# Gate and up projections of a routed feed-forward: scaled tokens, or coefficients applied to unscaled pieces

## The chip, the cores and the metric

The kernel runs on one NeuronCore of one Trainium2 chip. The metric is the device time of the program in microseconds (us). Each kernel is run several times and the median counts; one further execution is profiled. The engines are TensorE (PE in the profile, its weight loads PEld), VectorE (DVE), ScalarE (ACT), GpSimd (POOL) and SyncE (SP), which here only issues DMAs. PE writes to PSUM, which has eight banks of 512 fp32 columns.

## The reference

Two layers work on x (8 batches of 64 tokens of width 256, 512 tokens in all) with a context of 8 x 1601 rows. Each layer has cross-attention to the context, then (layer 0) a small attention and a top-1 routed ffn, or (layer 1) a state-space scan with gelu and a top-2 routed feed-forward. The change is in the last one:

```python
def _moe_linear(x, router_w, expert_w):
    logits = x @ router_w.T
    vals, idx = jax.lax.top_k(logits, K)
    probs = jax.nn.softmax(vals, axis=-1)
    onehot = jax.nn.one_hot(idx, n_exp, dtype=x.dtype)
    combine = jnp.einsum('tk,tke->te', probs, onehot)
    for e in range(n_exp):
        out = out + combine[:, e:e + 1] * (x @ expert_w[e].T)
g = _moe_linear(xt, router_gate, w_gate)      # 8 experts, 256 -> 1024
u = _moe_linear(xt, router_up, w_up)          # 8 experts, 256 -> 1024
inter = jax.nn.silu(g) * u
d = _moe_linear(inter, router_down, w_down)   # 8 experts, 1024 -> 256
```

All eight experts are computed for all tokens; the combine coefficient is zero for those not chosen.

## The kernel before

Semaphores are written out by hand, and each engine has its own in-order program. Precision is kept by splitting operands into a high and a low fp16 part (`wh`, `wl` for weights, times 256), and three matmuls stand for one product: high x high, high x low, low x high.

Attention runs over 16 groups g (8 batches in each of 2 layers), each with 13 steps k, one per 128 context rows. PE's units of a step stand in `STEP_UNITS`: S is the score of the step, P a bound on the maximum, K and V the projections of the next or own batch, W the weighing of values two steps back. ACT takes the exponentials of the scores (L1103), DVE the maxima (L1346). Group 15, the last, has no next batch, so its steps hold S, W and its own V units only. Between the units, `events(g, k)` puts the single operations of the middle work (output projection, norms, small attention, ffn of layer 0, scan, routers) of each tile of 128 tokens: `MID` and `SSM` name the operation for each step counted from step `MID_START` = 6 of a tile's first group. The scan's gelu (`s_y`) needs another ACT function table than the exponential, so two table loads stand around it. The last token tile (t = 3) can only follow group 15: its chain stands in `TAIL`.

The routed feed-forward of layer 1:
- `scale_tokens` (POOL, L649) multiplies the tokens of a tile by the coefficient of an expert; `transpose_tokens` (PE, L824) turns them; `split_tokens` (ACT L1121, DVE L1380) makes the fp16 parts `xch`, `xcl`. This is done for 2 routers x 8 experts x 4 tiles, in the 40 items of `X`.
- A unit (r, it) is gate (r = 0) or up (r = 1) for 128 of the 1024 output columns: weights are stationary, 512 tokens move, and the 8 experts with 2 halves of 256 and 3 products add up in one PSUM bank, 48 matmuls. Four gate units are done in parts ahead of the last tile, in the gaps of its chain (`gate_part`, items g and d of `TAIL`); the other 12 run in the loop at L995.
- `inner` (ACT, L1253) and the loop at L1595 (DVE) form silu from PSUM: exp, add one, reciprocal, times gate, times up; ACT and POOL (L711) split the result into `ih`, `il`, which have the intermediate columns on partitions as the down product wants them.
- Each weight block is 1 MB, loaded by SP to one of three buffers `w32` and split by ACT (`wh`, L1118) and DVE (`wl`, L1377) into a ring of four.
- Down: for each expert and tile 24 matmuls of 256 columns (L1031); DVE adds them into x with the coefficient (L1630).

PE's matmuls nearly all go through one helper, L717.

Of the kernel before, what the change touches and what calls it, by code (L numbers as in the profile page):

```python
# [7 lines left out]
F16 = mybir.dt.float16  # L8
# [8 lines left out]
B = 8  # L17
# [65 lines left out]
MID_START = 6  # L83
# [26 lines left out]
GATE_PARTS = [(n, e, *tiles) for units, tiles in (((0, 1), (0, 2)), ((0, 1), (2, 3)), ((2,), (0, 2)), ((2,), (2, 3)),  # L110
                                                  ((3,), (0, 2)), ((3,), (2, 3))) for n in units for e in range(E)]
LAST_GATE_PARTS = [(n, e, 3, 4) for n in range(GATES) for e in range(E)]

TAIL = ("x5 g g x6 y5 g y6 g x7 g y7 h2 out x8 h3 g g g g g y8 s_norm s_turn l2 g s_u x9 g s_0 y9 x10 g s_1 y10 x11 g "
        "s_2 y11 x12 g s_3 y12 x13 g s_4 y13 x14 g s_5 y14 x15 s_y y15 x16 g g g g g_stats y16 x17 g g g g g_norm "
        "g g g g g_parts g_clean m_stats y17 g g g g g m_norm m_turn l3 g r_logits g g g g g g g g g g g r_pick").split()
for e in range(E):
    TAIL += ["g"] * min(2, len(GATE_PARTS) - TAIL.count("g")) + [f"x{X_THIRD + e}", f"y{X_THIRD + e}"]  # L120
TAIL += ["g"] * (len(GATE_PARTS) - TAIL.count("g"))
TOKENS_AT = dict(zip((1, 3, 5, 7, 9, 15, 17, 19, 21, 23, 25, 27, 29, 30), range(X_BOTH, len(X))))
for n in range(len(LAST_GATE_PARTS)):
    TAIL.append("d")
    if n in TOKENS_AT:
        TAIL += [f"x{TOKENS_AT[n]}", f"y{TOKENS_AT[n]}"]
    if n == 9:
        TAIL += [f"h{GATES}", f"l{GATES}"]
for w in range(GATES + 1, 2 * GATES):
    TAIL += [f"h{w}", f"l{w}"]  # L130

UNITS = [(0, it) for it in range(GATES)] + [(1, it) for it in range(GATES)] + \
        [(r, it) for it in range(GATES, IT) for r in range(2)]
W_RING = 4


def events(g, k):
# [135 lines left out]
def build(nc, d, out):  # L273
    with ExitStack() as ctx:
# [18 lines left out]
        with ExitStack() as s:  # L293
            xg = sb(s, "xg", [P, 2, 2, D])
# [9 lines left out]
        small = sb(ctx, "small", [P, 32])  # L304
# [17 lines left out]
        SM_IOTA, SM_MIX, SM_HEAD, SM_FOLD = 2, 10, 18, 24  # L322
# [28 lines left out]
        with ExitStack() as s:  # L351
# [6 lines left out]
            xm = sb(s, "xm", [P, TT, D])  # L358
# [1346 lines left out]
```

## Time and profile before

| | before |
|---|---|
| time, median of 3 runs | 997.72 us (995.42 to 998.7) |
| profiled execution, its own time | 995.52 us |
| its span, first to last instruction | 993.7 us |
| PE / DVE / ACT / POOL busy | 925.3 / 606.9 / 535.0 / 202.1 us |
| mean granted TensorE clock | 0.986 |
| HBM read, written | 64.88 MB, 17.32 MB |

The profile gives busy time by engine, groups of instructions by line and shape, the chain of waits that ended last, and timelines. A matmul's record ends when its result is out, so consecutive matmuls overlap in the records: their price is the distance between starts. PEclk or clock is the granted TensorE clock as a share of 2.4 GHz; 0.5 is 1.2 GHz.

### The profile page before, as it was taken

What the parts mean: (1) busy time and instruction counts of PE and PEld (TensorE: products, weight loads), DVE (VectorE), ACT (ScalarE), POOL (GpSimd) and SP (SyncE); (2) the same over time, 40 slices, a digit from 0 to 9 for tenths busy, and PEclk for the clock granted to TensorE, in tenths of its full rate; (3) what the DMA queues carried; (4) which work ended last, traced back from release to release, by engine and by line L of the source; (5) the groups of instructions that cost most, each with busy time, mean ns of one, the idle gap of its engine ahead of it and who ended that gap; (6) DMA issues with size and microseconds to landing.
All of it is one profiled execution on the core that took longest, in us unless ns stands there. A gap on an engine that the chain in (4) does not pass through costs nothing.

```text
span 993.7 us, 35153 instructions
## 1 busy us (share of the span) xinstructions
PE 925.3 (93%) x15320; PEld 611.8 (62%) x15320; DVE 606.9 (61%) x1039; ACT 535.0 (54%) x1025; POOL 202.1 (20%) x233
## 2 busy tenths in 40 slices
PE   5579889999999999999999998998899999999998
PEld 2256556656656665666665665666778544446887
DVE  6556665767576466667765866775764774435422
ACT  5367766677676766656575666655735522112100
POOL 4211122121111212112121221313546100000000
PEclk9799999999999999999999999999899999999999
DMA  8677485553735442454344344324220432232100
GB/s 307 204 233 237 104 263 133 156 178 100 198 92 146 143 128 66 130 122 132 91 128 122 94 134 129 81 58 155 88 83 18 156 128 84 89 123 86 43 1 22
DMA packets 70843, 123.83 MB, mean 125 GB/s; under 512 B 34770, under 2 KB 46082, under 8 KB 67428
## 3 DMA queue, kind: packets, MB, share of 16 engines
q1 hardware_dynamic: 69812, 119.84, 40.4%
q8 instruction: 123, 2.02, 0.8%
q0 software_dynamic: 592, 1.42, 0.4%
q10 hardware_dynamic: 288, 0.33, 0.1%
q14 instruction: 28, 0.23, 0.1%
HBM read 64.88 MB, written 17.32 MB: 83 GB/s over the span
## 4 chain that ended last, share of the span: by engine, by line
PE 74%; ACT 9%; DVE 7%; issue 4%; SPq 3%; DMA 2%; POOL 1%; ACTq 0%; POOLq 0%; DVEq 0%
PE ps L717 72%; ACT p L1103 4%; SPq L472 3%; DVE mpart L1346 2%; DVE cl L1325 1%; ACT k L1086 1%; ACT kh L1087 1%; PE ps L837 1%; DMA c32b<-in_ctxT 1%; ACT ch L1070 1%; POOL xg L658 1%; PE ps L867 1%; DMA ks<-kh 1%; DVE wl L1377 0%; ACT L1103 0%
## 5 line engine op out<-in xcount | busy, mean ns | idle before, releaser
L1346 DVE TENSOR_REDUCE mpart<-ps 128x2 f32<-128x800 f32 (+1 forms) x256 | 252.4, 989 | 145.0 <-PE ps L717 144.0
L1103 ACT ACTIVATE p<-ps 128x512 f32<-128x512 f32 (+1 forms) x416 | 225.7, 596 | 180.0 <-PE ps L717 178.9
L646 POOL TENSOR_TENSOR kl<-k,kh 128x400 f16<-128x400 f32 (+1 forms) x128 | 120.1, 939 | 445.0 <-ACT kh L1087 445.0
L717 PE MATMUL ps<-p,v 128*17 128x64 f32 x6656 | 133.3, 224 | 0.0
L717 PEld LDWEIGHTS ps<-p,v 128*17 128x17 f32 x6656 | 99.6, 99 | 37.5 <-issue 36.0
L717 PE MATMUL ps<-wvh,ch 128*128 128x256 f16 (+1 forms) x416 | 114.5, 275 | 0.8 <-issue 0.8
L717 PE MATMUL ps<-wvh,cl 128*128 128x256 f16 (+1 forms) x416 | 113.4, 273 | 0.0
L717 PE MATMUL ps<-wvl,ch 128*128 128x256 f16 (+1 forms) x416 | 113.4, 273 | 0.0
L717 PE MATMUL ps<-xcl,wh 128*128 128x512 f16 (+2 forms) x384 | 112.8, 308 | 0.0
L717 PE MATMUL ps<-xch,wh 128*128 128x512 f16 (+2 forms) x384 | 112.7, 308 | 0.0
L717 PE MATMUL ps<-xch,wl 128*128 128x512 f16 (+2 forms) x384 | 112.7, 308 | 0.0
L717 PE MATMUL ps<-ch,wkh 128*128 128x400 f16 (+1 forms) x256 | 88.0, 344 | 19.6 <-ACT kh L1087 17.0
L717 PEld LDWEIGHTS ps<-qcur,ks 64*128 64x128 f16 (+1 forms) x3328 | 61.9, 97 | 67.5 <-issue 50.8
L1377 DVE SCALAR_TENSOR_TENSOR wl<-w,wh 128x2048 f16<-128x2048 f32 x24 | 54.8, 2291 | 79.1 <-ACT wh L1118 79.1
L717 PE MATMUL ps<-kh,qbcur 64*128 64x400 f16 (+1 forms) x512 | 86.6, 335 | 15.8 <-DVE mpart L1346 12.5
L717 PE MATMUL ps<-qcur,ks 64*128 64x64 f16 (+1 forms) x3328 | 86.2, 192 | 12.1 <-ACT p L1103 8.2
L717 PE MATMUL ps<-cl,wkh 128*128 128x400 f16 (+1 forms) x256 | 86.9, 340 | 0.0
L717 PE MATMUL ps<-ch,wkl 128*128 128x400 f16 (+1 forms) x256 | 86.5, 338 | 0.0
L1118 ACT ACTIVATE wh<-w 128x2048 f16<-128x2048 f32 x24 | 45.5, 1902 | 59.4 <-PE ps L717 59.4
L717 PE MATMUL ps<-wh,ih 128*128 128x256 f16 x256 | 69.8, 273 | 0.0
L717 PE MATMUL ps<-wl,ih 128*128 128x256 f16 x256 | 69.8, 273 | 0.0
L717 PE MATMUL ps<-wh,il 128*128 128x256 f16 x256 | 69.8, 273 | 0.0
(210 smaller groups left out, 1390.0 us busy)
## 6 DMA issues: line engine op xcount, KB each, us to landing
ks<-kh SPq DMA_DIRECT2D x256, 100.1 KB
w<-in_wgu SPq DMA_DIRECT2D x16, 1024.0 KB, 4.9
ks<-kl SPq DMA_DIRECT2D x128, 100.1 KB
w<-in_wd SPq DMA_DIRECT2D x8, 1024.0 KB, 4.8
c32a<-in_ctxT SPq DMA_DIRECT2D x16, 400.5 KB, 5.1
cparts<-ch SPq DMA_DIRECT2D x8, 800.5 KB, 6.2
cparts<-cl SPq DMA_DIRECT2D x8, 800.5 KB, 8.1
c32a<-in_ctxT SPq DMA_DIRECT2D x12, 400.0 KB, 3.3
```

The costliest lines, as they stand in the source:

```text
L472: sp.dma_start(dst, src).then_inc(sem(name), 16)
L646: nc.gpsimd.tensor_tensor(kl[:, mt, k0:k0 + w], k32[:, ku % 2, 0:w], kh[:, mt, k0:k0 + w], ALU.subtract).then_inc(sem("klo_done"), 1)
L658: ins = nc.gpsimd.tensor_scalar(xg[:, i % 2, t - t0, :], xm[:, t, :], cmb[:, TT * r + t, e:e + 1], None, ALU.mult)
L717: return nc.tensor.matmul(o, lhsT, rhs, start=start, stop=stop, skip_group_check=shared)
L837: last = nc.tensor.transpose(o, xg[:, i % 2, t, P * kc:P * kc + P], ident[:, :])
L867: last = nc.tensor.transpose(mid[:, P * kc:P * kc + P], src[:, P * kc:P * kc + P], ident[:, :])
L1070: nc.scalar.activation(ch[u][:, kc, k0:k0 + w], c32[s][:, 0:w], ACT.Copy).then_inc(sem("chi_done"), 1)
L1086: nc.scalar.activation(k32[:, i % 2, 0:w], o[:, 0:w], func, **how).then_inc(sem("k32_done"), 1)
L1103: nc.scalar.activation(p32[0:n, step % PRING, BANK * side:BANK * side + BANK], ps[0:n, side, :], ACT.Exp, scale=DH ** -0.5).then_inc(sem(" ...
L1118: nc.scalar.activation(wh[:, w % W_RING, :], w32[:, w % 3, :], ACT.Copy, scale=W_SCALE)\
L1346: nc.vector.reduce_max(mpart[:, j0:j0 + 3:2, quarter], o.rearrange("p (b c) -> p b c", b=2)[:, :, 0:w], AX.X).then_inc(sem("max_done"), 1)
L1377: nc.vector.scalar_tensor_tensor(wl[:, w % W_RING, :], w32[:, w % 3, :], W_SCALE, wh[:, w % W_RING, :], ALU.mult, ALU.subtract).then_inc(s ...
```

## The change

Tokens are no longer scaled. The normed tokens of a tile are turned and split once (`xmh`, `xml`). A weight block is now one expert's whole gate or up matrix (256 x 1024), and the work is cut into 128 pieces: (weight block, tile t, half h of the 1024 columns). A piece has the tokens of the tile stationary and 512 weight columns moving, 6 matmuls into one of four PSUM banks (4 to 7). DVE (or ACT for 10 of the pieces that are a tile's first) multiplies the piece by the expert's coefficient per token and adds it into `acc` in SBUF. Silu is formed from `acc` by exponential (ACT) and add, reciprocal and multiply (DVE), for 8 pieces of 512 columns, at places written out in `TAIL`. The intermediate now has tokens on partitions, so PE turns it (32 fp32 transposes, `turn_intermediate`), ACT takes the high part and DVE the low part. The weight ring has 8 places. The first six pieces stand in steps 7 to 12 of group 15, 20 in the chain of the last tile, the others behind it; after piece 127 comes the down product in the order `DOWN`. The logits of the down router are formed with tokens on the output partitions (64 matmuls of 16 columns) in place of 16 matmuls of 512 columns and a transpose. `MID_START` goes from 6 to 3, so the middle work of all tiles stands three steps earlier. `scale_tokens`, `transpose_tokens`, `split_tokens`, `gate_part` and `inner` are gone.

```diff
...
-MID_START = 6
+MID_START = 3
...
+SPLIT_AT = {(G - 1, 6): 0, (G - 1, 9): 1}
+PIECES_AT = {(G - 1, k): k - 7 for k in range(7, KT)}
...
+UNITS = [(0, 0), (1, 0)] + [(0, e) for e in range(1, E)] + [(1, e) for e in range(1, E)]
+GATES_DONE = UNITS.index((0, E - 1)) + 1
+AHEAD = 6
+PIECES = [(w, t, h) for w in range(AHEAD) for t in range(TT - 1) for h in range(2)] + \
+        [(w, TT - 1, h) for w in range(AHEAD) for h in range(2)] + \
+        [(w, t, h) for w in range(AHEAD, 2 * E) for t in range(TT) for h in range(2)]
+W_RING = 8
+W_EARLY = 5
+HF = FI // 2
...
+def first_by_act(q):
+
+    w, t, h = PIECES[q]
+    return UNITS[w][1] == 0 and (UNITS[w][0] == 1 or t == TT - 1)
...
+CHAIN = [("out", 2), ("s_norm", 0), ("s_turn", 1), ("s_u", 1), ("s_0", 1), ("s_1", 1), ("s_2", 1), ("s_3", 1), ("s_4", 1),
+         ("s_5", 1), ("s_y", 2), ("g_stats", 1), ("g_norm", 1), ("g_parts", 1), ("g_clean", 1), ("m_stats", 1),
+         ("m_norm", 0), ("m_turn", 1), ("r_logits", 2), ("r_pick", 0)]
+CHAIN_SPLITS = {"s_norm": 2, "s_2": 3, "s_5": 4, "m_norm": 5, "r_pick": 6}
+CHAIN_HIGHS = {"out": 2, "s_0": 3, "s_3": 4, "s_y": 5, "m_turn": 6}
...
+for name, n in CHAIN:
+    TAIL.append((name, TT - 1))
+    if name in CHAIN_HIGHS:
+        TAIL.append(("h", CHAIN_HIGHS[name]))
+    if name in CHAIN_SPLITS:
+        TAIL.append(("l", CHAIN_SPLITS[name]))
+    for _ in range(n):
+        add_part()
...
+catch_up = AHEAD * 2 * (TT - 1)
+while True:
+    q = add_part()
+    w, t, h = PIECES[q]
+    if q == catch_up + 3:
+        TAIL += [("h", 7), ("l", 7)]
+    if q == catch_up + 2 * AHEAD - 1:
+        TAIL += [("h", 8), ("l", 8)]
+    if w >= AHEAD and (t, h) == (1, 1):
+        TAIL += [("h", w + 3), ("l", w + 3)]
+    n = q - (len(PIECES) - 8 * (2 * E - GATES_DONE)) - 4
+    if n >= 0 and n % 6 == 0 and n // 6 < 2 * TT:
+        TAIL.append(("silu", n // 6))
+    if q == len(PIECES) - 2 * TT - 1:
+        break
+for j in range(2 * TT):
+    q = len(PIECES) - 2 * TT + j
+    TAIL += [("g", q)] + ([("v", q - 1)] if j == 0 else [])
+    TAIL += [("v", q), ("i", j)]
+    if j >= 3:
+        TAIL.append(("turn", j - 3))
+    if j >= 3:
+        TAIL.append(("low", j - 3))
+    if j == 3:
+        TAIL += [("h", 18), ("l", 18)]
+DOWN = [(0, 0), "5", (0, 1), "6", (1, 0), "7", (1, 1), (0, 2), (0, 3), (1, 2), (1, 3)] + \
+       [(e, t) for e in range(2, E) for t in range(TT)]
+LAST_TURNS = (5, 6, 7)
...
+            def part(q):
+
+                w, t, h = PIECES[q]
+                if q == 0:
+                    pe.wait_ge(sem("v_done"), V_UNITS * G)
                     pe.wait_ge(sem("max_done"), 2 * NP * G)
-                    pe.wait_ge(sem("row_done"), G)
-                elif i == X_SECOND:
+                if q >= 4:
+                    pe.wait_ge(sem(part_out(q - 4)[0]), part_out(q - 4)[1])
+                if (t, h) == (0, 0):
+                    pe.wait_ge(sem("wlo_done"), w + 1)
+                pe.wait_ge(sem("xml_ready"), t + 1)
+                tokens = slice(P * t, P * t + P)
+                for kc in range(KC):
+                    c = slice(FI * kc + HF * h, FI * kc + HF * h + HF)
+                    for m, (a, b_) in enumerate(((xmh, 0), (xmh, 1), (xml, 0))):
+                        last = mm(ps[:, part_bank(q), :], a[:, kc, tokens], w16(w, b_)[:, c], kc == 0 and m == 0,
+                                  kc == KC - 1 and m == 2)
+                last.then_inc(sem("part_mm"), 1)
...
+            def turn_intermediate(j):
+
+                pe.wait_ge(sem("inter"), j + 1)
+                if j == 0:
                     pe.wait_ge(sem("exp_done"), 2 * KT * G)
-                pe.wait_ge(sem(f"xg_ready{i % 2}"), i // 2 + 1)
-                need(pe, "xcl_ready", i - 1)
-                for t in range(t1 - t0):
-                    for kc in range(KC):
-                        o = ps[:, token_bank(i), P * (2 * kc + t):P * (2 * kc + t) + P]
-                        last = nc.tensor.transpose(o, xg[:, i % 2, t, P * kc:P * kc + P], ident[:, :])
-                last.then_inc(sem("xcT_mm"), 1)
-
-            def gate_part(n, e, t0, t1):
-
-                if e == 0 and t0 == 0:
-                    pe.wait_ge(sem("wlo_done"), n + 1)
-                    if n == 0:
-                        pe.wait_ge(sem("v_done"), V_UNITS * G)
-                if n == 0:
-                    pe.wait_ge(sem("xcl_ready"), X.index((0, e, t0, t1)) + 1)
-                tokens = slice(P * t0, P * t1)
-                for kc in range(KC):
-                    c = (kc * E + e) * P
-                    for m, (a, b_) in enumerate(((wh, xch), (wh, xcl), (wl, xch))):
-                        last = mm(ps[:, gate_bank(n), tokens], a[:, n, c:c + P], b_[0][:, e, kc, tokens],
-                                  e == 0 and kc == 0 and m == 0, e == E - 1 and kc == KC - 1 and m == 2)
-                return last
+                need(pe, "ilo_done", j - 1)
+                for n in range(IT // 2):
+                    last = nc.tensor.transpose(ps[:, j % 2, P * n:P * n + P], i32[:, j % 2, P * n:P * n + P], ident[:, :])
+                last.then_inc(sem("iT_mm"), 1)
...
-            def scale_tokens(i):
-
-                r, e, t0, t1 = X[i]
-                if i == 0:
-                    pool.wait_ge(sem("k_mm"), K_UNITS * B)
-                    pool.wait_ge(sem("v_mm"), V_UNITS * B)
-                pool.wait_ge(sem("cmb_done"), t1)
-                need(pool, "xcT_mm", i - 1)
-                for t in range(t0, t1):
-                    ins = nc.gpsimd.tensor_scalar(xg[:, i % 2, t - t0, :], xm[:, t, :], cmb[:, TT * r + t, e:e + 1], None,
-                                                  ALU.mult)
-                ins.then_inc(sem(f"xg_ready{i % 2}"), 1)
...
+            def part_first(q):
+
+                act.wait_ge(sem("part_mm"), q + 1)
+                act.wait_ge(sem("cmb_done"), PIECES[q][1] + 1)
+                nc.scalar.activation(part_acc(q), ps[:, part_bank(q), :], ACT.Copy, scale=part_coefficient(q))\
+                   .then_inc(sem("first_out"), 1)
...
+            def gate_exponential(j):
+
+                t, h = j // 2, j % 2
+                act.wait_ge(sem("part_out"), part_out(max(q for q in range(len(PIECES)) if PIECES[q] ==
+                                                          (GATES_DONE - 1, t, h)))[1])
+                if j == 0:
+                    act.wait_ge(sem("pv_mm"), KT * G)
+                need(act, "gated", j - 1)
+                nc.scalar.activation(sg[:, j % 2, :], acc[:, 0, t, HF * h:HF * h + HF], ACT.Exp, scale=-1 / W_SCALE)\
+                   .then_inc(sem("sg"), 1)
...
+            def intermediate_high(j):
+
+                act.wait_ge(sem("iT_mm"), j + 1)
+                nc.scalar.activation(turned(ih, j), ps[:, j % 2, :].rearrange("p (i c) -> p i c", c=P), ACT.Copy)\
+                   .then_inc(sem("ihi_done"), 1)
...
+            def part_add(q):
+
+                w, t, h = PIECES[q]
+                r, e = UNITS[w]
+                dve.wait_ge(sem("part_mm"), q + 1)
+                to, o = part_acc(q), ps[:, part_bank(q), :]
+                if e == 0:
+                    if q == 0:
+                        dve.wait_ge(sem("clo_done"), 4 * B)
+                        dve.wait_ge(sem("f_mm"), 4 * TT)
+                    ins = nc.vector.tensor_scalar(to, o, part_coefficient(q), None, ALU.mult)
+                else:
+                    before = part_out(PIECES.index((UNITS.index((r, e - 1)), t, h)))
+                    dve.wait_ge(sem(before[0]), before[1])
+                    ins = nc.vector.scalar_tensor_tensor(to, o, part_coefficient(q), to, ALU.mult, ALU.add)
+                ins.then_inc(sem("part_out"), 1)
...
+            def gate(j):
+
+                t, h = j // 2, j % 2
+                g_acc = acc[:, 0, t, HF * h:HF * h + HF]
+                dve.wait_ge(sem("sg"), j + 1)
+                link(nc.vector.tensor_scalar(sg[:, j % 2, :], sg[:, j % 2, :], 1.0, None, ALU.add))
+                link(nc.vector.reciprocal(sg[:, j % 2, :], sg[:, j % 2, :]))
+                nc.vector.tensor_tensor(g_acc, sg[:, j % 2, :], g_acc, ALU.mult).then_inc(sem("gated"), 1)
...
+            def intermediate(j):
+
+                t, h = j // 2, j % 2
+                c = slice(HF * h, HF * h + HF)
+                dve.wait_ge(sem("part_out"), part_out(len(PIECES) - 2 * TT + j)[1])
+                dve.wait_ge(sem("gated"), j + 1)
+                need(dve, "iT_mm", j - 1)
+                nc.vector.scalar_tensor_tensor(i32[:, j % 2, :], acc[:, 1, t, c], 1 / (W_SCALE * W_SCALE),
+                                               acc[:, 0, t, c], ALU.mult, ALU.mult).then_inc(sem("inter"), 1)
...
+            def intermediate_low(j):
+
+                dve.wait_ge(sem("ihi_done"), j + 1)
+                nc.vector.tensor_tensor(turned(il, j), ps[:, j % 2, :].rearrange("p (i c) -> p i c", c=P),
+                                        turned(ih, j), ALU.subtract).then_inc(sem("ilo_done"), 1)
...
```

In the programs of PE, ACT and DVE, `TAIL` is walked in order: g is `part` on PE, v is `part_first` on ACT or `part_add` on DVE, h and l are the two halves of a weight split, silu, i, turn and low are the functions above; the other names are the chain's events.

## Rows read from the trace of the kernel before

**Rows 1.** Page: busy us, share of the span, instructions.

```profile
PE 925.3 (93%) x15320; PEld 611.8 (62%) x15320; DVE 606.9 (61%) x1039; ACT 535.0 (54%) x1025; POOL 202.1 (20%) x233
```

**Rows 2.** Chain of waits in time: start, length, engine, tile, line.

```profile
773.08 1.83 POOL xg L658 x2
...
776.39 214.68 PE ps L717 x1374
```

**Rows 3.** Timeline of PE: start, length, line, operation, tiles, shapes.

```profile
904.26 0.38 PE L717 MATMUL ps<-xcl,wh 128*128 128x512 f16 x1
904.48 0.38 PE L717 MATMUL ps<-xch,wl 128*128 128x512 f16 x1
```

**Rows 4.** Timeline of PE: scores (15,0) and (15,7), last weighing.

```profile
677.02 0.41 PE L717 MATMUL ps<-qcur,ks 64*128 64x64 f16 x16 [0.57 <-DMA ks<-kh]
...
695.57 0.61 PE L717 MATMUL ps<-qcur,ks 64*128 64x64 f16 x16
...
708.73 1.91 PE L717 MATMUL ps<-p,v 128*17 128x64 f32 x64
```

**Rows 5.** Groups by form, 776 to 994: count, busy us, mean ns, idle.

```profile
L717 PE MATMUL ps<-xch,wh 128*128 128x512 f16 x192 | 72.8, 379 | 0.0
...
L717 PE MATMUL ps<-wh,ih 128*128 128x256 f16 x256 | 69.8, 273 | 0.0
...
L1377 DVE SCALAR_TENSOR_TENSOR wl<-w,wh 128x2048 f16<-128x2048 f32 x19 | 43.4, 2291 | 75.3 <-ACT wh L1118 75.3
...
L1601 DVE RECIPROCAL sg<-sg 128x512 f32<-128x512 f32 x8 | 26.8, 3353 | 0.3
...
L1630 DVE SCALAR_TENSOR_TENSOR x<-ps,cmb,x 128x256 f32<-128x256 f32 x32 | 13.5, 477 | 29.5 <-PE ps L717 29.5
...
L1606 DVE SCALAR_TENSOR_TENSOR i<-ps,sg 128x512 f32<-128x512 f32 x8 | 5.5, 692 | 6.8 <-PE ps L717 6.7
```

**Rows 6.** Timeline of DVE: a silu unit, then adds of two experts.

```profile
853.83 2.29 DVE L1377 SCALAR_TENSOR_TENSOR wl<-w,wh 128x2048 f16<-128x2048 f32 x1 [7.46 <-ACT wh L1118]
856.04 0.42 DVE L1600 TENSOR_SCALAR sg<-sg 128x512 f32<-128x512 f32 x1
856.50 3.35 DVE L1601 RECIPROCAL sg<-sg 128x512 f32<-128x512 f32 x1
859.88 0.69 DVE L1602 TENSOR_TENSOR sg<-sg,ps 128x512 f32<-128x512 f32 x1
...
943.01 1.65 DVE L1630 SCALAR_TENSOR_TENSOR x<-ps,cmb,x 128x256 f32<-128x256 f32 x4
...
953.49 1.65 DVE L1630 SCALAR_TENSOR_TENSOR x<-ps,cmb,x 128x256 f32<-128x256 f32 x4
```

**Rows 7.** Groups by form, 683 to 776.4: transposes of scaled tokens.

```profile
L837 PE MATMUL ps<-ident,xg 128*128 128x128 f32 x128 | 22.5, 290 | 2.8 <-POOL xg L658 1.5 <-DVE xcl L1385 1.3
```

**Rows 8.** Timeline of PE: output projection and two scan steps of the last tile.

```profile
715.22 1.89 PE L717 MATMUL ps<-wo,oT 128*128 128x256 f32 x8
...
723.01 0.43 PE L717 MATMUL ps<-st_s,am 64*64 64x126 f32 x2
...
724.39 0.42 PE L717 MATMUL ps<-st_s,am 64*64 64x124 f32 x2
```

**Rows 9.** Timeline of DVE: last tile, from statistics to norm.

```profile
731.28 0.43 DVE L1292 BATCH_NORM_STATS2 st<-g_a 128x6 f32<-128x256 f32 x1 [0.21 <-ACT g_a L1211]
...
738.70 0.41 DVE L1299 TENSOR_SCALAR xm<-x,mv,rstd 128x256 f32<-128x256 f32 x1
```

**Rows 10.** By stretch: width, busy PE, PEld, DVE, ACT, POOL; clock, DMA, GB/s.

```profile
537.00:541.00 4.00, 1.56 (x8) 0.60 (x6) 1.09 (x2) 2.38 (x5) 0.89 (x1) 0.87 1.00 353
541.00:545.00 4.00, 4.00 (x91) 2.40 (x94) 1.10 (x2) 2.29 (x5) 0.78 (x1) 0.70 0.10 35
...
705.00:710.00 5.00, 3.90 (x104) 3.30 (x106) 3.67 (x9) 4.41 (x7) 1.03 (x1) 0.50 0.43 180
```

**Rows 11.** Timeline of ACT: the first weight split in group 15.

```profile
698.88 1.91 ACT L1118 ACTIVATE wh<-w 128x2048 f16<-128x2048 f32 x1
```

More of the change, by code:

```diff
@@ L112 @@
[L112 to L133, printed above, removed]
@@ new lines, with part_out @@
+W_EARLY = 5
[3 more added lines that the diff above has]
+    return UNITS[w][1] == 0 and (UNITS[w][0] == 1 or t == TT - 1)
+def part_out(q):
+    if first_by_act(q):
+        return "first_out", sum(first_by_act(p) for p in range(q + 1))
+    return "part_out", sum(not first_by_act(p) for p in range(q + 1))
+CHAIN = [("out", 2), ("s_norm", 0), ("s_turn", 1), ("s_u", 1), ("s_0", 1), ("s_1", 1), ("s_2", 1), ("s_3", 1), ("s_4", 1),
+         ("s_5", 1), ("s_y", 2), ("g_stats", 1), ("g_norm", 1), ("g_parts", 1), ("g_clean", 1), ("m_stats", 1),
+         ("m_norm", 0), ("m_turn", 1), ("r_logits", 2), ("r_pick", 0)]
@@ new lines, with add_part @@
+CHAIN_SPLITS = {"s_norm": 2, "s_2": 3, "s_5": 4, "m_norm": 5, "r_pick": 6}
+CHAIN_HIGHS = {"out": 2, "s_0": 3, "s_3": 4, "s_y": 5, "m_turn": 6}
+TAIL = [("v", len(PIECES_AT) - 1), ("g", len(PIECES_AT))]
+def add_part(lag=1):
+    q = sum(item[0] == "g" for item in TAIL) + len(PIECES_AT)
+    TAIL.append(("g", q))
+    if q - lag > max(item[1] for item in TAIL if item[0] == "v"):
+        TAIL.append(("v", q - lag))
+    return q
+for name, n in CHAIN:
[6 more added lines that the diff above has]
+        add_part()
@@ L623, in _ @@
                             load(w32[:, w, :], weight(w), f"w_in{w}")
-            for w in range(3, 2 * IT + E):
-                sp.wait_ge(sem("wlo_done"), w - 2)
-                load(w32[:, w % 3, :], weight(w), f"w_in{w % 3}")
+                    if (g, k) in ((G - 1, 8), (G - 1, 11)):
+                        load_weight(3 + k // 11)
+            for w in range(5, 3 * E):
+                load_weight(w)
             for t in range(TT):
@@ L703, in _ @@
                         event(name, layer, t)
[L704 to L712 removed]
+            for name, _ in CHAIN:
+                event(name, 1, TT - 1)
         @block.tensor
@@ L1113, in split_w @@
                     act.wait_ge(sem("v_mm"), V_UNITS * G)
+                elif w == W_EARLY:
+                    act.wait_ge(sem("main_mm"), 2 * KT * G)
                 elif w >= W_RING:
                     unit = w - W_RING
-                    act.wait_ge(sem("gu_mm"), min(unit + 1, 2 * IT))
-                    need(act, "d_mm", unit + 1 - 2 * IT)
-                nc.scalar.activation(wh[:, w % W_RING, :], w32[:, w % 3, :], ACT.Copy, scale=W_SCALE)\
+                    last = max(q for q in range(len(PIECES)) if PIECES[q][0] == unit)
+                    act.wait_ge(sem("part_mm"), last + 1)
@@ L1612, in _ @@
-            split_w(2 * IT + W_RING - 1)
-            dve.wait_ge(sem("ld_mm"), 1)
-            link(nc.vector.tensor_copy(lgm[:, 2 * TT:3 * TT, :],
-                                       ps[:, 0, 0:E * TT].rearrange("p (t e) -> p t e", t=TT)))
+            for name, n in TAIL:
+                if name == "l":
+                    split_w(n)
+                elif name == "v":
+                    if not first_by_act(n):
+                        part_add(n)
+                elif name == "silu":
+                    gate(n)
+                elif name == "i":
+                    intermediate(n)
+                elif name == "low":
+                    intermediate_low(n)
+                elif name not in ("h", "g", "turn"):
+                    event(name, 1, n)
```

342 lines of the change are left out of this document (128 added, 214 removed).

## Prediction

> **What bounds the kernel now.** I read the page first: TensorE (PE) is busy 925.3 of 993.7 us, VectorE (DVE) 606.9 [rows 1]. PE is the engine to follow, and the place where the change acts is after the last weighing of values, where the expert products (FFN) run. The chain of waits says that the last stretch with any wait is the scaling of tokens on POOL and their transposes; from 776.39 on there is nothing but PE for 214.68 us, to 991.07 [rows 2]. So until the end the price is PE's matmul count times its spacing. The timeline gives the spacing: 0.216 us for 512 columns [rows 3]. Here the Trainium skill, page "TensorE: Matmul & The Clock Gate", section "Back-to-back issue gap", gives about 131 ns for such a sustained stream; by it a block of six matmuls would take an estimated 0.79 us, not the 1.29 used below. The row decides, and the sum goes by it.
>
> The last weighing begins at 708.73 and ends at 710.6 [rows 4]. From there to PE's last matmul are 280.5 us. The two halves below are "before 710.6" and "after 710.6".
>
> **Gate and up columns.** They stay. Before, 16 units of 48 matmuls of 512 columns (12 units are seen as 3 x 192 in [rows 5]); after, 128 pieces of 6. One piece is 6 x 0.2157 = 1.294 us, all of them 165.6 us either way. The down product stays too: 768 matmuls of 256 columns (3 x 256 in [rows 5]); an expert takes 953.49 - 943.01 = 10.48 us [rows 6], eight take 83.9.
>
> **What is removed from PE.** The transposes of scaled tokens, 128 of them for 22.5 us of busy time, with the waits for POOL around them [rows 7]; with these gone, PE's own work behind 710.6 would be some 20 us shorter if nothing else waited. POOL's scaling, ACT's and DVE's splits of scaled tokens go as well, all of them beside PE.
>
> **What is added, and where the gain goes.** DVE now adds every piece from PSUM into SBUF, except 10 that ACT takes. An add is a scalar_tensor_tensor of 512 columns with a coefficient per partition. The nearest row is L1630, the same form over 256 columns: 477 ns, and four of them in 1.65 us, so (1.65 - 0.475)/3 = 0.39 us from start to start [rows 5, 6]. A 2048-column split ends 2.29 us after its start and the next starts after 2.21, so 256 more columns are about 0.27 us: an add costs 0.66 us. The other DVE costs: split 2.21 (853.83 to 856.04); one silu piece (add one, reciprocal 3.35, multiply) from 856.04 to 859.88 + 0.61 = 4.45 us [rows 6]; the product into i32 and the new subtraction for the low half 0.61 each, from 692 ns [rows 5].
>
> While no silu is due, a weight unit of 8 pieces costs DVE 8 x 0.66 + 2.21 = 7.5 us against PE's 10.4: hidden. But the order written out by hand puts the eight silu pieces at pieces 76, 82 ... 118. From piece 74 to the start of the down product DVE has in its queue: 52 adds 34.3, 8 silus 35.6, 7 splits 15.5, 5 products 3.1, 3 low halves 1.8: together 90 us. PE in the same stretch has 53 pieces and 5 turns, 68.6 + 2.5 = 71 us. A piece may not start until the add four pieces back is done (four PSUM banks), so PE can be three pieces ahead and no more: DVE is the bound there, and PE stands 19 us. Should the clock fall to its lower level in those gaps, most of it is hidden, since PE waits there anyway; 0 to 4 us, and I take 0. In the kernel before, the same reciprocals (8 x 3.35 = 26.8 [rows 5]) lay beside PE.
>
> Behind 710.6, after the change:
> - pieces 6 to 74, 69 x 1.294 = 89.3.
> - the last tile's chain on PE: output projection 1.7 (recorded 1.89), scan steps at 0.45 each (0.43 and 0.42 recorded [rows 8]) 2.7, the others 2.4: 6.8. A link took 1.38 us from 723.01 to 724.39 [rows 8]; with a 1.29 us piece between, it is 1.76, so the scan's latency is covered.
> - waits inside that chain: 0.9 before the first transpose. From gelu's statistics to the norm DVE took 7.8 us, 731.28 to 739.1 [rows 9]; now five adds and a wait for piece 17 stand in it, 13 us by my queue, against 9.1 us of pieces: 2.9 us. A split behind s_2 delays a scan by 0.5. Router choice and one split before add 26: 1.6. With 0.9 of small ones: 6.8.
> - DVE's stretch 90, and 1 for DVE waiting on pieces where no split falls between two silus.
> - down 83.9; three turns left over 1.5; the router of the down product as 64 matmuls of 16 columns: nearest from below 0.41/16 x 64 = 1.6 (a score matmul, [rows 4]), from above 7 at the 0.109 of a 256-column matmul; I take 2.5, near the short one.
> Sum 281.8, against 280.5: +1.3. So the whole 20 us go into DVE's queue.
>
> **What is moved.** MID_START 6 to 3 puts each tile's middle work three steps earlier. It loads ACT's gelu tables at step 0, not step 3, for the tiles in groups 11, 13 and 15. At step 3 ACT's two table loads delay keys that PE needs at once: in 537 to 541 PE is busy 1.56 of 4 us, and the clock in 537 to 545 is at 0.87 and 0.70, that is 3.4 us at 1.2 in place of 2.4 GHz, after PE stood: 2.4 + 1.7 = 4.1 us [rows 10], and the same again near 615. At step 0 three value units and two max units (5.5 us of PE) stand before the next scores that need ACT. Together up to 8.1; I take 6.5, since other work now falls on the busy steps 4 and 5. What that could cost no row shows; from 0 to the same 8.1 I let it reach.
>
> **Group 15.** (15,7) began at 695.57 [rows 4]. The gelu stall and three token transposes leave, 3.3 us; pieces 0 to 5 (7.8 us) come in at steps 7 to 12, where a step is 0.9 + 1.3 = 2.2 us and scores no longer wait for ACT. But piece 0 waits for weight 0: ACT's split of 1.91 [rows 11] and DVE's 2.29 behind step 6, a 3.4 us stand, and the clock was at 0.50 in 705 to 710 after such stands [rows 10]. End of the weighing by this count: 710.4 + 1.7 = 712.1, that is +1.5.
>
> **Sum.** -6.5 + 1.5 + 1.3 = -3.7, rounded -3.5. The profiled execution: span 993.7, own time 995.5, becomes 990.2 and 992.0. That execution lies 2.2 below the median of the runs, 997.7; forecast for the median 994.2.
>
> **Rivals.**
> - VectorE is not the bound. If PE ran through the late pieces as in the early ones, 19 us less: 975. For it: DVE is busy only 61% of the span [rows 1]. Against it: 3353 ns in all 8 reciprocals, and the order fixed in the code. 0.08.
> - The shift saves nothing, the slower side: the expert-bias and gate work of layer 0 and the first transposes now meet steps 4 and 5, where ACT must hand keys to PE (the 2.4 us above was such a wait). It decides from the point where these stalls cost more than 3.5 us back; with all 6.5 gone, 1001 (998 to 1005). 0.22.
> - DVE instructions do not overlap: 75 instructions in the late stretch at 0.08 us more, +6, 1000. Against it: starts 2.21 apart for a duration of 2.29 [rows 6]. The Trainium skill says this, page "VectorE: DVE Perf Modes", section "The DRAIN you can't avoid": the next operation starts only when the pipe is empty. The rows show a small overlap, so by this trace it is unlikely for instructions without a dependence. 0.10.
> - The shift gives all of its 8.1 and the clock holds in group 15: 994.2 - 1.6 - 1.7 = 991, and to 985 if the chain's waits close too. 0.15.
> The forecast itself 0.45, own range 990 to 999.
>
> **How the numbers follow.** The range 985 to 1004 leaves out the first rival and the far ends of the second. A difference under 0.3% (3 us) can't be told from none. Faster: 0.08 + 0.15 + half of 0.45 = 0.46. Slower: half of the second and third, and a little of the forecast, 0.22. Same: 0.32.
>
> **What would show it.** In the profile after: adds with 0.66 us between starts; DVE above 95% busy for 85 to 90 us, in that stretch PE idle near 19 us in waits for DVE's adds, in gaps of 1 to 3 us at each silu; no table-load stall in groups 11 and 13; a wait of about 3 us before the last tile's final transpose and one before piece 0; POOL nearly idle at the end. I would be wrong by most if DVE's late stretch is not full, or if groups 2 to 10 change their length by more than 1 us each.

## The result and the profile after

The changed kernel took 1004.66 us (median of 6 runs, 1000.54 to 1006.12) against 997.6 of the kernel before: ratio 1.0066, 95% interval 1.0044 to 1.0089. In a second comparison on another occasion it was 1.0074 (1.0053 to 1.0094). The forecast was 994.2, range 985 to 1004. Of the experiments below, one execution of before_l1 took 1297 us at a clock of 0.655 and stays out of its ratio.

Page of after (busy us, share, instructions), to be read against [rows 1]:

```profile
PE 913.3 (91%) x14880; PEld 577.8 (58%) x14880; DVE 670.6 (67%) x1129; ACT 519.8 (52%) x984; POOL 142.3 (14%) x175
```

PE is 12 us less busy and the profiled execution 10 us longer: PE's idle time grew. DVE gained 64 us.

Each kernel was traced twice (runs before_again and after_again are the second traces). Stretches of PE in us (scores (g,0) as in [rows 4]):

| Stretch | before | after | change (means) | forecast |
|---|---|---|---|---|
| start to (1,0) | 93.0, 95.5 | 95.6, 94.6 | +0.9 | 0 |
| (1,0) to (9,0) | 346.3, 347.2 | 352.5, 354.2 | +6.6 | 0 |
| (9,0) to (15,0) | 237.7, 236.5 | 231.0, 231.0 | -6.1 | -6.5 |
| (15,0) to end of last weighing | 33.6, 31.6 | 36.2, 35.9 | +3.4 | +1.5 |
| from there to PE's last matmul | 280.4, 281.1 | 286.1, 286.1 | +5.4 | +1.3 |

The last row of after has three parts, the same in both traces: to the start of piece 75 101.7 (forecast 102.9), from there to the start of the down product, the late stretch, 96.6 (91), and from there 87.8 (87.9). So one part of the tail is off, a little of group 15, and one stretch far ahead of both.

Late stretch of after by windows (width, busy PE, PEld, DVE, ACT, POOL; clock, DMA share, GB/s):

```profile
817.00:837.00 20.00, 16.88 (x70) 7.00 (x69) 17.87 (x17) 3.71 (x4) 0.00 (x0) 0.91 0.14 52
837.00:857.00 20.00, 15.59 (x70) 6.41 (x68) 19.86 (x20) 1.85 (x3) 0.00 (x0) 1.00 0.30 106
857.00:877.00 20.00, 16.00 (x73) 7.00 (x74) 19.64 (x21) 5.43 (x5) 0.00 (x0) 1.00 0.15 53
877.00:897.00 20.00, 16.12 (x72) 6.61 (x70) 19.86 (x19) 0.00 (x0) 0.00 (x0) 1.00 0.30 105
897.00:914.00 17.00, 13.36 (x59) 6.80 (x60) 14.56 (x21) 4.28 (x6) 0.00 (x0) 0.83 0.18 63
```

PE is idle 19.05 of 97 us and DVE is full in the three middle rows. What PE waits for there (us in total, times, longest):

```profile
PE ps L748 <- DVE acc L1398: 16.3, 10, 2.7
PE ps L881 <- DVE il L1423: 2.6, 2, 2.3
```

Timeline of DVE in after, one silu (start, length, idle before):

```profile
821.15 3.35 DVE L1407 RECIPROCAL sg<-sg 128x512 f32<-128x512 f32 x1
824.54 0.69 DVE L1408 TENSOR_TENSOR acc<-sg,acc 128x512 f32<-128x512 f32 x1
825.15 2.72 DVE L1398 SCALAR_TENSOR_TENSOR acc<-ps,cmb,acc 128x512 f32<-128x512 f32 x4
828.27 0.75 DVE L1398 SCALAR_TENSOR_TENSOR acc<-ps,cmb,acc 128x512 f32<-128x512 f32 x1 [0.40 <-PE ps L748]
830.44 0.75 DVE L1398 SCALAR_TENSOR_TENSOR acc<-ps,cmb,acc 128x512 f32<-128x512 f32 x1 [1.42 <-PE ps L748]
```

Four adds in 2.72 us, each 0.75 long: 0.66 from start to start, as forecast. The last two rows are what was not forecast: DVE, the bound, waits for PE, 1.8 us in all. PE's timeline and windows say why:

```profile
825.95 0.60 PE L748 MATMUL ps<-w16a,xmh 128*128 128x512 f16 x2 [2.34 <-DVE acc L1398]
...
828.02 1.06 PE L748 MATMUL ps<-w16a,xmh 128*128 128x512 f16 x2
...
830.88 0.59 PE L748 MATMUL ps<-w16a,xmh 128*128 128x512 f16 x2
```

```profile
827.00:832.00 5.00, 5.00 (x18) 1.98 (x17) 3.15 (x6) 0.76 (x1) 0.00 (x0) 0.71 0.00 0
...
897.00:902.00 5.00, 3.91 (x11) 1.48 (x12) 4.93 (x8) 0.00 (x0) 0.00 (x0) 0.66 0.00 0
```

Behind a stand of 2.34 us the first matmuls are still quick (two in 0.60), then the same ones come at half the pace (two in 1.06), then at 0.59 again; the granted clock of 827 to 832 is 0.71, a mix of 2.4 and 1.2 GHz.

Group 15 of after by windows, same columns, and what piece 0 waits for:

```profile
693.00:699.00 6.00, 2.13 (x72) 1.54 (x59) 2.99 (x5) 4.30 (x7) 0.00 (x0) 0.81 0.00 0
699.00:704.00 5.00, 4.75 (x57) 2.28 (x58) 2.96 (x16) 1.29 (x3) 0.00 (x0) 0.54 0.62 213
```

```profile
PE ps L748 <- DVE w16a L1381: 3.8, 1, 3.8
```

Piece 0 stands 3.8 us for weight 0, and the next 5 us run at 0.54; by an estimate from these figures that takes 5 x 0.46 = 2.3 us more.

The gelu tables of group 11 now load three steps earlier, where PE has other work. Timeline of ACT and windows of after; the kernel before had its two loads at 534.35 and 536.04, and the windows to compare with are the first two of [rows 10]:

```profile
531.67 1.28 ACT L1229 ACT_TABLE_LOAD   x1
...
533.67 1.28 ACT L1108 ACT_TABLE_LOAD   x1 [0.33 <-PE ps L748]
```

```profile
529.00:533.00 4.00, 4.00 (x75) 2.94 (x72) 1.92 (x4) 2.42 (x5) 0.95 (x1) 1.00 0.28 61
533.00:537.00 4.00, 4.00 (x77) 2.92 (x75) 3.60 (x8) 2.71 (x4) 0.00 (x0) 1.00 0.62 149
537.00:541.00 4.00, 3.82 (x117) 2.38 (x116) 3.52 (x6) 2.17 (x4) 0.00 (x0) 1.00 0.52 121
```

PE is full during the loads and busy 3.82 of 4 us behind them, where the kernel before had 1.56, and the clock stays at 1.00.

### The profile page after: what moved, and what is told of

The parts are those of the page before. It is cut to its first block, busy times and chain, and to the rows that moved or that the text cites. A ratio compares the mean times of both kernels' runs of the same rounds, so it can differ in the third digit from the quotient of the medians.

```text
span 1004.0 us, 34414 instructions
## 1 busy us (share of the span) xinstructions
PE 913.3 (91%) x14880; PEld 577.8 (58%) x14880; DVE 670.6 (67%) x1129; ACT 519.8 (52%) x984; POOL 142.3 (14%) x175
## 4 chain that ended last, share of the span: by engine, by line
PE 65%; DVE 17%; ACT 6%; issue 5%; SPq 4%; DMA 2%; POOL 0%; DVEq 0%; ACTq 0%
PE ps L748 64%; SPq L523 4%; DVE acc L1398 3%; ACT p L1108 3%; DVE sg L1407 3%; DVE mpart L1350 2%; DMA c32b<-in_ctxT 1%; DVE cl L1329 1%; ACT ch L1075 1%; DVE w16a L1381 1%; ACT kh L1092 1%; ACT k L1091 1%; DVE v L1341 1%; PE ps L894 1%; DMA qbscratch<-qb 1%
## 5 line engine op out<-in xcount | busy, mean ns | idle before, releaser
L748 PE MATMUL ps<-p,v 128*17 128x64 f32 x6656 | 130.7, 221 | 0.0
L748 PEld LDWEIGHTS ps<-p,v 128*17 128x17 f32 x6656 | 97.3, 97 | 37.0 <-issue 36.1
L748 PE MATMUL ps<-w16a,xmh 128*128 128x512 f16 x320 | 97.5, 387 | 11.9 <-DVE acc L1398 8.0
L1398 DVE SCALAR_TENSOR_TENSOR acc<-ps,cmb,acc 128x512 f32<-128x512 f32 x112 | 79.5, 745 | 13.5 <-PE ps L748 13.4
L748 PE MATMUL ps<-w16b,xmh 128*128 128x512 f16 x192 | 58.8, 389 | 10.0 <-DVE acc L1398 9.9
L748 PE MATMUL ps<-w16a,xml 128*128 128x512 f16 x160 | 61.8, 386 | 0.0
L748 PEld LDWEIGHTS ps<-w16a,xmh 128*128 128x128 f16 x320 | 30.0, 99 | 50.1 <-DVE acc L1398 11.0
L748 PE MATMUL ps<-w16a,ih 128*128 128x256 f16 x320 | 53.5, 275 | 0.0
L1341 DVE SCALAR_TENSOR_TENSOR v<-ps,rows 128x512 f32<-128x512 f32 (+1 forms) x56 | 36.3, 649 | 24.3 <-PE ps L748 23.3
L748 PEld LDWEIGHTS ps<-wvh,ch 128*128 128x128 f16 (+1 forms) x416 | 41.4, 100 | 17.4 <-issue 7.9
```

Of the source, the lines that this page charges most:

```text
L748: return nc.tensor.matmul(o, lhsT, rhs, start=start, stop=stop, skip_group_check=shared)
L1341: nc.vector.scalar_tensor_tensor(v[0:n, kts[0]:kts[-1] + 1, :, 0:DH], o[0:n, 0:D * len(kts)].rearrange("p (k h d) -> p k h d", h=H, d=DH), ...
L1398: ins = nc.vector.scalar_tensor_tensor(to, o, part_coefficient(q), to, ALU.mult, ALU.add)
```

## The experiments

Each kernel ran in turn with the kernel before on the same chip, and the ratios (95% interval in brackets) are to that one. Medians and changes are in us; changes are against the changed kernel's medians of 1004.3 and 1004.7 or before's of 996.5 to 997.6.

### Is DVE's queue the bound of the late stretch?

**norecip**, the changed kernel without the reciprocals:

```diff
-                link(nc.vector.reciprocal(sg[:, j % 2, :], sg[:, j % 2, :]))
```

> The changed kernel without the eight reciprocals of silu on VectorE (this part of silu is left out; add, multiply and all else stay). Theory D (VectorE's queue bounds the stretch from piece 74 to the down product): 8 x 3.35 = 26.8 us leave VectorE, 91.7 become 65, below TensorE's 77.6, so TensorE's idle of 18 to 20 us there goes: 985 to 988. Rival (the stretch is bound by chains from engine to engine or by the clock rather than by VectorE's sum): less than 10 us less, 995 or more.

Measured 982.6 (ratio 0.9854, 0.9820 to 0.9888). The late stretch takes 74.2 us in place of 96.6: theory D. Not all of these 22.4 us are the queue itself. PE is full here and its clock 1.00 (one window of the stretch below), and with the clock at 1.00 the changed kernel's stretch took 93.2 in another run (start6, below); so about 19 us are the queue and 3.4 the clock.

```profile
836.00:856.00 20.00, 20.00 (x94) 9.06 (x93) 17.05 (x22) 4.86 (x4) 0.00 (x0) 1.00 0.31 106
```

**lnexp** computes all of silu, with its inverse as exp(-ln(1+e)) on ScalarE:

```diff
-                   .then_inc(sem("sg"), 1)
+                   .then_inc(sem("sg_step"), 1)
+                act.wait_ge(sem("sg_step"), 2 * j + 1)
+                nc.scalar.activation(sg[:, j % 2, :], sg[:, j % 2, :], ACT.Ln, bias=1.0).then_inc(sem("sg_step"), 1)
+                act.wait_ge(sem("sg_step"), 2 * j + 2)
+                nc.scalar.activation(sg[:, j % 2, :], sg[:, j % 2, :], ACT.Exp, scale=-1.0).then_inc(sem("sg"), 1)
...
-                link(nc.vector.tensor_scalar(sg[:, j % 2, :], sg[:, j % 2, :], 1.0, None, ALU.add))
-                link(nc.vector.reciprocal(sg[:, j % 2, :], sg[:, j % 2, :]))
```

> The changed kernel with silu's 1/(1+e) computed on ScalarE as exp(-ln(1+e)): add and reciprocal leave VectorE (8 x 3.84 = 31 us of its queue), three activations of 0.63 us in place of one go to ScalarE, and at most two table loads of 1.28 each time. Theory D (VectorE's queue is the bound): the stretch from piece 75 to the down product takes 75 to 80 us in place of 96.6, the whole 980 to 986, as without the reciprocal (982.6). Rival (ScalarE's longer chain, with loads of tables and the splits of weights behind it, becomes the bound): over 85 us there, 990 or more.

Measured 983.15 (0.9867, 0.9844 to 0.9889), 21.1 less than the changed kernel beside it, and the late stretch again takes 74.2. Its windows:

```profile
819.00:839.00 20.00, 20.00 (x95) 9.05 (x93) 17.19 (x21) 14.01 (x14) 0.00 (x0) 1.00 0.30 106
839.00:859.00 20.00, 20.00 (x94) 9.04 (x93) 16.41 (x20) 13.56 (x16) 0.00 (x0) 1.00 0.28 106
859.00:879.00 20.00, 20.00 (x94) 9.11 (x93) 17.04 (x21) 6.14 (x6) 0.00 (x0) 1.00 0.31 105
879.00:893.20 14.20, 11.37 (x62) 6.00 (x60) 12.54 (x17) 4.08 (x5) 0.00 (x0) 1.00 0.21 74
```

PE is full in the first three rows and the clock 1.00; PE's work in the stretch sums to 71.37, the forecast's 71. ACT pays, but has the room (timeline of lnexp):

```profile
823.40 0.63 ACT L1143 ACTIVATE sg<-acc 128x512 f32<-128x512 f32 x1 [5.75 <-DVE acc L1410]
824.04 1.28 ACT L1146 ACT_TABLE_LOAD   x1
825.34 0.63 ACT L1146 ACTIVATE sg<-sg 128x512 f32<-128x512 f32 x1
825.99 1.28 ACT L1148 ACT_TABLE_LOAD   x1
827.28 0.63 ACT L1148 ACTIVATE sg<-sg 128x512 f32<-128x512 f32 x1
```

**before_lnexp** makes the same edit in the kernel before.

> The kernel before with the same edit of silu (exp(-ln(1+e)) on ScalarE, no add and no reciprocal on VectorE). Theory D says that what the reciprocals cost depends on where they stand: here they lie beside TensorE's products, which nothing holds up. So no difference from before, within 1.5 us, although VectorE is some 30 us less busy. Rival (the reciprocals cost time wherever they are, or the new silu is a gain of its own): 5 us less or more, and then the gain of 21 us in the changed kernel could not be put down to its own queue.

Measured 996.5 (0.9995, 0.9979 to 1.0012), with DVE at 577.2 us busy in place of 606.9. So the same reciprocals cost nothing there (2 us at most, by the interval), and 21 us with the clock's share here.

### Two more traces

> The kernel before, once more, for a second trace of it. Theory L (the single profiled execution of before was a favourable one: the kernels run so far whose code is the same up to group 9 are 2 to 3 us later at group 1 and another 3.5 later at group 9, in single steps of 0.8, 1.5 and 2.6 us): the second trace reaches the scores of group 1 one to three us later than 92.95 and takes 348 to 350 us from group 1 to group 9 in place of 346.3. Rival M (the new layout of buffers costs something in every group): 92.9 and 346.3 again within 0.5.

> The changed kernel, once more, beside the kernel before on the same chip. Its ratio to before should come out at 1.007 to 1.009 again. Theory L: its second trace differs from the first by steps of 0.8 to 2.6 us at single places. From piece 75 to the down product 93 to 97 us, since that stretch measured 96.6, 93.2 and 94.7 in the three traces so far that keep the reciprocals.

Measured: before_again 995.8 (1.0003, 0.9981 to 1.0025), after_again 1004.3 (1.0074, 1.0053 to 1.0094) with 96.6 in the late stretch. M falls for the start, where (1,0) came at 95.5. L holds there, and less in the groups, which took 347.2 where 348 to 350 were expected. Where the code is equal, two traces follow each other to 0.01 us in most steps and part at single ones: the two of before by 1.86 us in group 0 and by 0.82 from (2,1) to (2,2), where the clock is 1.00 in both. So one trace is good to 2 or 3 us up to a milestone.

### The shift of MID_START

The starts of each version, in summary (layer 1's has its own constant where the two differ):

```text
 start6       MID_START = 6                            # changed kernel
 split36      layer 0 at 6, layer 1 at 3               # changed kernel
 before3      MID_START = 3                            # kernel before
 before_l0    layer 0 at 3, layer 1 at 6               # kernel before
 before_l1    layer 0 at 6, layer 1 at 3               # kernel before
 combo_stair  layer 0's four tiles at 6, 5, 4, 3       # combo, below
```

> The changed kernel with MID_START back at 6, all else kept. Theory S (the shift costs in layer 0 what it gives in layer 1): the scores of group 12 start some 4 us earlier than in the changed kernel (its excess over the kernel before was +4.1 there), and from group 11 to the scores of group 15 some 4 to 6 us are lost again to the gelu table loads; the time is 1004 to 1006, unchanged within 2 us. Theory R (the early excess has another cause, such as where buffers lie or the run itself, and the shift is worth the 6.5 us that were forecast): groups 0 to 10 keep their excess and the time is 1010 to 1012.

> The changed kernel with two starts in place of one: layer 0's middle work at step 6 as before, layer 1's at step 3. Theory S: both gains at once, group 10 starts within 2 us of the kernel before and groups 11 to 14 keep their 6.7 us gain: 997 to 1000. Theory R: no change against the changed kernel's 1004.7 within 2 us, since the early excess stays.

> The kernel before with MID_START at 3 and nothing else. Theory S: 0 plus or minus 2 us against its 997.6, with groups 2 to 8 longer by 5 to 6 us in sum and groups 9 to 14 shorter by 6 to 7. Theory R: 991.

Measured: start6 1012.3 (1.0139, 1.0099 to 1.0179), split36 1004.4 (1.0084, 1.0055 to 1.0112), before3 992.6 (0.9952, 0.9930 to 0.9973). Theory S, which I had read off the two traces, falls: by the medians the shift is worth 7.6 us in the changed kernel and 4.1 in the kernel before (4.8 by the ratio, interval 2.7 to 7). R is nearer. How the shift splits between the layers was left open.

> The kernel before with layer 0's middle work at start 3 and layer 1's left at 6. Theory L0 (start 3 costs about 3 us in layer 0): 998 to 1001, 2 to 4 us over before's 996.8, and the traces of groups 11 and 13 keep the stands behind the gelu table loads. Rival (start 3 costs nothing in layer 0; what the traces show there is work brought forward): within 1 us of before.

> The kernel before with layer 1's middle work at start 3 and layer 0's left at 6, so that the last tile of layer 0 and the first of layer 1 overlap by three steps more. The shift of both gave 4.1 us. Theory L0: the gain of layer 1, 6 to 8 us, is here without layer 0's cost, less what the overlap takes (2.7 in group 10 and 2.1 in group 12 in the changed kernel with these starts): 992 to 995. Rival: the overlap takes all, 996 or more.

Measured: before_l0 1000.4 (1.0027, 1.0008 to 1.0045), 2.7 us slower by the ratio. before_l1 993.5 (0.9967, 0.9947 to 0.9987), 3.3 faster by the ratio. Of what layer 1 gives, the overlap of the last tile of layer 0 with the first of layer 1 takes 2.3 us back, from (10,0) to (11,0) in its trace. With both halves shifted the overlap is the old one: -4.8 by the ratio, so with +2.7 for layer 0, layer 1 is worth about 7.5 if the two halves simply add up. The forecast had 8.1 at most for groups 11 and 13, and the gelu stall of group 15 in another term.

The cost in layer 0 falls in group 2. There (2,0) to (3,0) took 43.2 and 44.0 us in the traces of before and 48.7 in that of before_l0. All 16 traces that have one start for layer 0 agree: nine with start 3 took 45.6 to 50.5 us there (mean 47.6), seven with start 6 43.2 to 44.3 (mean 43.8), and from (3,0) to (10,0) the means are 306.1 and 305.9. From (1,0) to (10,0) that makes 395.5 against 391.5. So the +6.6 of the table, cut at (9,0), overstates this cost: the traces together say 4.0, before_l0's time 2.7. PE's waits in group 2 (us in total, times, longest), first of before, then of before_l0:

```profile
PE ps L717 <- DVE mpart L1346: 1.6, 2, 0.9
PE ps L717 <- issue: 0.8, 1, 0.8
```

```profile
PE ps L718 <- issue: 2.8, 2, 2.1
PE ps L907 <- DVE a_mT L1458: 1.8, 1, 1.8
```

The wait for a_mT is new; a wait behind issue stands in both traces of before too (0.8 and 1.6). A further part goes with the clock, in the traces where it fell. Windows of before, then of before_l0 at the start of the group:

```profile
134.00:178.00 44.00, 41.23 (x878) 27.54 (x877) 26.30 (x43) 28.89 (x59) 7.89 (x9) 1.00 0.67 198
```

```profile
136.60:147.00 10.40, 8.27 (x157) 5.79 (x156) 5.13 (x10) 3.75 (x7) 0.00 (x0) 0.88 0.93 304
147.00:152.00 5.00, 5.00 (x102) 3.51 (x96) 3.37 (x6) 3.42 (x6) 0.00 (x0) 0.91 0.37 73
```

With start 6 the clock of group 2 was 1.00 in all seven traces. With start 3 it was 1.00 in four (before3, norecip, late_pieces, combo_late2: 45.6 to 47.0 us) and 0.93 to 0.97 in five (47.9 to 50.5). Why only the first tile pays, no run settles.

> As the version with both edits, with the starts of layer 0's middle work at steps 6, 5, 4 and 3 for its four tiles in place of 3 for all; layer 1's stay at 3. In the traces with start 3 the way from the scores of group 1 to those of group 10 took 393.7 to 398.6 us, in those with start 6 390.2 to 393.3. Theory L0 (start 3 costs about 3 us in layer 0, and the version with starts 6 and 3 gained nothing because the last tile of layer 0 then overlapped with the first of layer 1): 2 to 4 us less than the version with both edits. Rival (what start 3 costs there is given back where the tiles end): the same within 1 us.

Measured: combo_stair 986.5 (0.9893, 0.9869 to 0.9917), 5.4 slower than combo. The first tile, at step 6, gained 4.4 us against combo from (2,0) to (3,0); then 10.8 were lost up to (8,0), 10.0 of them in groups 4 to 7, where the tiles at 5 and 4 stand. So both L0 as stated there and its rival miss: the cost is not smooth in the start; 5 and 4 are worse than 3 and 6.

### Group 15

```diff
-PIECES_AT = {(G - 1, k): k - 7 for k in range(7, KT)}
+PIECES_AT = {(G - 1, k): k - 8 for k in range(8, KT)}     # late_pieces, and start6_late
```

> The changed kernel with the first piece one step later: five pieces at steps 8 to 12 of group 15 in place of six at steps 7 to 12, the sixth behind the weighing. Theory W (piece 0 stands 3.8 us for the split of weight 0, and the clock then falls): from the scores of group 15 to the end of its weighing 36.2 becomes 31 to 33 (one piece of 1.3 less and 2 to 4 of waiting), the whole is 2 to 3 us faster than the changed kernel. Rival (the time in group 15 is VectorE's adds and ScalarE's exponentials in turn): 34.9, no change of the whole within 1 us.

Measured: 1001.3 (1.0052, 1.0034 to 1.0070), 3.0 faster by the medians and 2.2 by the ratios, with group 15 in 32.4. As theory W has it, the wait for w16a is gone from PE's list, and the 5 us around and behind piece 0 have clock 0.80, not 0.54:

```profile
697.00:702.00 5.00, 5.00 (x87) 2.31 (x79) 2.79 (x18) 3.03 (x6) 0.00 (x0) 0.80 0.60 210
```

> The changed kernel with MID_START at 6 and the first piece one step later. At start 6 and with six pieces group 15 took 42.6 us to the end of its weighing, at start 3 36.2 and 35.9. Theory G (the extra 6.5 us are the gelu table loads of the third tile meeting the pieces, one full stand of ScalarE behind the other, wherever piece 0 is): about 39 to 40 here, 3 less as at start 3, and 1009. Rival (the extra comes from piece 0 itself, whose tokens and weight are late at start 6): 34 to 36, and 1004 or less.

Measured: 1005.6 (1.0098, 1.0071 to 1.0125), group 15 in 36.7. That is near the rival's 34 to 36 and below G's 39 to 40, but in neither range. The later piece is worth 6.7 us by the medians and 4.1 by the ratios at start 6, against 2 to 3 at start 3. With the late piece the shift gives 1005.6 - 1001.3 = 4.3, about as in the kernel before; what it gave the changed kernel beyond that was this collision.

**combo** (lnexp and late_pieces) and **combo_late2** (another step later):

> The changed kernel with both edits: silu's reciprocal by ln and exp on ScalarE, and the first piece one step later. If the two costs are independent, 1004.3 - 21.1 - 3.0 = 980.2, 979 to 982. If the second was only a matter of where the clock fell, it adds nothing here: 983.

> As the version with both edits, with the first piece a second step later (four pieces in group 15, at steps 9 to 12). Piece 0 stood for weight 0 until 1 us behind step 7; at step 8 it still stood 1.7 more than a piece takes. Theory W (only the wait for weight 0 counts): no further gain, within 1 us, since one more piece moves behind the weighing at its full 1.3. Rival (each piece inside group 15 costs more than its 1.3 us, because scores and exponentials wait in turn): another 1 to 2 us less.

Measured: combo 981.0 (0.9835, 0.9811 to 0.9859), 16 us faster than the kernel before, with everything computed. The two edits add up: 23.3 of the 24.1 us expected. combo_late2 983.5 (0.9859, 0.9838 to 0.9880): no gain, by the medians a loss of 2.5, which neither theory had. In its trace the step that lost its piece has PE waiting 2.05 us for ACT's exponentials, and group 15 took 33.8 us against combo's 32.3, though it holds one piece less.

## Why the prediction was wrong

- **What was right.** The gain of the removed transposes did go into DVE's queue, as forecast: DVE was 91.7 us busy (forecast 90), and PE idle 19.05 (19), mostly behind adds. norecip, lnexp and before_lnexp show it. That the 19 was met so closely is partly luck, since PE's work took 77.6 us with the lower clock in it, not 71. The rival "VectorE is not the bound" is out; what it promised (19 us) is what lnexp fetched (21, of which 3.4 are the clock's).
- **The failed step: "Should the clock fall ... most of it is hidden ... 0 to 4 us, and I take 0".** It was not hidden. A piece must be done before its add, and with PE at 1.2 GHz DVE ran out of finished pieces and waited. start6's late stretch, same instructions, had clock 1.00 in all its windows and took 93.2, with DVE 91.6 busy; after had 0.91 and 0.83 at its ends and took 96.6, with DVE as busy and waiting more. The other traces with the reciprocals lie between or near: split36 and late_pieces 94.7 at a mean clock of 0.98, start6_late 96.0 at 0.95, both of after 96.6 at 0.96. By an estimate, 0.96 over 96.6 us is 4.3 us of PE's work, of which 3.4 came out as time. First and last window of start6's:

```profile
826.00:846.00 20.00, 16.23 (x74) 6.86 (x72) 19.25 (x18) 4.86 (x4) 0.00 (x0) 1.00 0.15 52
...
906.00:919.50 13.50, 10.29 (x57) 5.56 (x56) 12.98 (x18) 4.08 (x5) 0.00 (x0) 1.00 0.22 79
```

  So 3.4 us are the clock. Of the other 2.2 (93.2 against 91), 1.6 are DVE's busy time, for the trace has 53 adds and 6 products where I counted 52 and 5, and 0.6 its short waits (1.6 against the 1 allowed). I had no row for taking the lower end of my 0 to 4, and it came out close to the upper one.
- **Second failed step, "What that could cost no row shows": layer 0.** The range for it ran from 0 to 8.1 and I took 1.6 for all of it. before_l0 measures 2.7 (0.8 to 4.5) for layer 0 alone, the traces together 4.0, nearly all in group 2. Layer 1's gain stood: -6.1 in the traces from (9,0) to (15,0), forecast -6.5, and the gelu stalls are gone from groups 11 and 13. The slow rival ("the shift saves nothing") named this cost, and its 998 to 1005 holds the result, but that is luck: by before3 the cost takes back about a third, not all, and it shows as a wait for DVE's a_mT, waits behind issue and a fallen clock, not as waits for keys.
- **Third, the size of group 15.** The wait for weight 0 was seen (3.4 us; measured 3.8) and so was the low clock (1.7; 2.3 by the estimate above), yet +1.5 was the sum and +3.4 came. One us of the difference is the trace the forecast was made from, whose own clock was low there: 33.6 us at a mean of 0.85, the second trace of before 31.6 at 1.00. late_pieces shows what was there to save.
- **The other terms.** Pieces 6 to 74 with chain and waits 101.7 (102.9); down product with turns and router 87.8 (87.9); add 0.66; the stand ahead of the last tile's final transpose 2.3 (2.9). DVE instructions do overlap, so that rival is out, with its +6. The rule of the Trainium skill that I set beside it ("VectorE: DVE Perf Modes", "The DRAIN you can't avoid") isn't seen for independent adds, which start 0.66 us apart at 0.75 long; the same section goes on that an operation that is not held starts earlier, and that agrees.
- **Sum.** Missing against -3.5: 2.7 (layer 0), 1.9 (group 15), 5.6 (late stretch), less 1.2 (pieces and chain), 9.0 in all, of 10 to 11 between forecast and result; with 4.0 for layer 0 it is 10.3. A rest of 1 to 2 us can't be told from the size of what a trace shows at random: both traces of after lie 1.2 and 2 above their medians, the trace the forecast was made from 2.1 below its own.

## What to carry to other kernels

When a change empties the bound engine and fills another's queue, add that queue up over the stretch where its work falls, not over the span: DVE, busy 67% of the changed kernel's span, was the bound for 97 us. Then ask which third engine is free there: the same eight reciprocals cost nothing beside full matmuls and 19 us in a full queue, 21 with the clock. And an engine that waits in small stands may come back at half clock: cost that too, where the bound engine needs its output within a few us.

## What the runs showed of the hardware

- TensorE's granted clock fell behind a stand of 2.34 us (0.71 from 827 to 832 in after). It did not fall behind the same stand in start6 (1.00 throughout), nor behind stands of 2.37 and 2.66 us later in the same trace of after (1.00 from 837 to 897). So the length of one stand does not decide it, and what does no run here shows. The falls go with the time of an execution: of the changed kernel's six, the fastest had a mean clock of 0.990 (1000.5 us), the slowest 0.980 (1006.1). They are not all of it, as the 0.82 us between the two traces of before at clock 1.00 shows.
- A switch of ACT's tables costs 1.28 us and nothing visible behind it: in lnexp the load starts at 824.04 and the next activation at 825.34. The Trainium skill ("ScalarE: Activation LUTs", "What ACT_TABLE_LOAD costs") gives the same 1283 ns for the load; the drain that it adds isn't seen. By its section "Table sets: the hidden batching unit" ln and exp share a set and want one load; here each silu loaded twice, 16 loads for 8.
- Inverting by ln and exp costs ACT 3.8 us more a piece with its two loads (2 x 0.63 + 2 x 1.28; ACT's busy time grows by 30.0 us in lnexp and 30.8 in before_lnexp for eight). DVE's add and reciprocal cost 3.8 too. The work is the same in length, and it is better placed where the engine is idle.
